# Layer 2 attention: ScalarE copies the projected queries out, high parts first in the scores, earlier folds, sums reordered, six block additions on VectorE

## The reference, cut to what matters

```python
xn = _layernorm(x)                                   # 8 x 512 x 128
# attention
xa = layernorm(xn, g1)
q = xa @ Wq.T                                        # 16 heads of 64
k, v = split(xa @ Wkv.T)                             # one head of 64, shared
q, k = l2norm(q * 16) * 4, l2norm(k) * 4
attn = softmax(causal(q @ k.T))                      # 16 x 512 x 512
x = x + layernorm((attn @ v) @ Wout.T, g2) + ffn(xn)
# ffn: (silu(xn @ Wg.T) * (xn @ Wu.T)) @ Wd.T, hidden 384
```

## Time and profile before

| what | value |
|---|---|
| time, median of 3 runs | 1253.22 us (1252.53 to 1253.65) |
| the profiled execution | 1259.26 us, its span 1257.5 us |
| PE, DVE, ACT, POOL busy in the span | 1158.6, 884.8, 670.3, 484.8 us |
| mean granted clock of TensorE | 0.978 of full speed |
| layer 2 | from about 622 us to the end, 8 turns |

### The profile page before, as it was taken

One profiled execution on the slowest core, in us unless ns is written; L12 is line 12 of the kernel. 1 busy time (PEld: TensorE's weight loads), 2 busy tenths in 40 slices (PEclk: granted clock), 3 DMA queues, 4 the chain that ended last, 5 costly groups with the idle time before them and its releaser, 6 DMA issues.

```text
span 1257.5 us, 26722 instructions
## 1 busy us (share of the span) xinstructions
PE 1158.6 (92%) x8667; PEld 789.6 (63%) x8667; DVE 884.8 (70%) x2425; ACT 670.3 (53%) x1290; POOL 484.8 (39%) x691
## 2 busy tenths in 40 slices
PE   5999999999999998898499999999999999999997
PEld 3656656665666654888365757657576575765755
DVE  7888888888888895554475767757677576775744
ACT  2766676667667655454263552635526355263550
POOL 5222212122222312553373572735727357273450
PEclk8999999999999998899699999999999999999998
DMA  3311112120101100222012030120301203012030
GB/s 91 100 47 39 56 26 57 27 70 17 27 17 27 26 10 1 55 58 51 10 23 39 13 54 6 23 38 13 54 4 25 38 13 54 4 25 38 9 52 9
DMA packets 43717, 42.31 MB, mean 34 GB/s; under 512 B 7040, under 2 KB 36224, under 8 KB 43648
## 3 DMA queue, kind: packets, MB, share of 16 engines
q0 software_dynamic: 11008, 17.31, 7.9%
q1 hardware_dynamic: 32640, 24.15, 7.1%
HBM read 13.72 MB, written 6.75 MB: 16 GB/s over the span
## 4 chain that ended last, share of the span: by engine, by line
issue 18%; PE 11%; POOL 7%; DMA 5%; ACT 5%; DVE 5%; POOLq 0%; ACTq 0%; DVEq 0%
DMA arena<-arena 5%; PE gather L496 4%; PE ring_a L496 3%; PE pair L496 3%; ACT arena L1510 3%; POOL arena L1286 3%; POOL arena L1207 2%; POOL q_len L1248 1%; DVE q_parts L1994 1%; POOL late L1286 1%; ACT arena L1490 1%; ACT q_parts L1498 1%; DVE arena L2068 1%; PE ring_d L496 1%; PE pair L500 1%
## 5 line engine op out<-in xcount | busy, mean ns | idle before, releaser
L1353 ACT ACTIVATE arena<-ring_a 128x384 f32<-128x384 f32 (+1 forms) x512 | 253.6, 550 | 148.4 <-PE ring_a L496 148.4
L1102 POOL TENSOR_SCALAR_AFFINE_SELECT arena<-arena 128x512 f32<-128x512 f32 x128 | 82.8, 647 | 367.5 <-ACT arena L1353 367.4
L496 PE MATMUL ring_a<-q_max,rows 128*128 128x384 f32 (+1 forms) x512 | 197.5, 389 | 2.2 <-DVE q_max L1659 1.8
L1645 DVE CUSTOM_DVE_ANT_0 arena<-pair,arena 128x384 bf16<-128x384 f32 (+1 forms) x269 | 161.0, 613 | 23.6 <-PE pair L496 19.2
L1510 ACT ACTIVATE arena<-ring_a 128x1024 f32<-128x1024 f32 x96 | 98.8, 1029 | 105.3 <-PE ring_a L496 105.3
L1248 POOL TENSOR_TENSOR q_len<-q_sum,exponents 128x8 f32<-128x8 f32 x64 | 105.5, 1649 | 111.3 <-DVE q_sum L1975 111.0
L496 PE MATMUL ring_a<-q_parts,k_rows 64*128 64x384 f32 (+2 forms) x1152 | 124.8, 339 | 16.0 <-DVE q_parts L1994 15.2
L496 PE MATMUL ring_a<-arena,v_aug 128*32 128x384 f32 (+1 forms) x1024 | 124.3, 557 | 1.7 <-POOL arena L1102 0.6
L496 PE MATMUL pair<-arena,v_aug 128*64 128x512 f32 (+3 forms) x768 | 114.0, 439 | 4.1 <-ACT arena L1510 3.5
L496 PEld LDWEIGHTS ring_a<-q_parts,k_rows 64*128 64x128 f32 x1152 | 92.2, 186 | 35.0 <-issue 15.8
L496 PE MATMUL pair<-rows,q_rows 128*128 128x384 f32 (+1 forms) x269 | 110.0, 411 | 3.4 <-DMA rows<-k_rows 2.6
(11 more groups left out here) (274 smaller groups left out, 2353.5 us busy)
## 6 DMA issues: line engine op xcount, KB each, us to landing
arena<-arena POOLq DMA_DIRECT2D x32, 384.0 KB, 4.4
rows<-k_rows SPq DMA_DIRECT2D x128, 64.0 KB, 2.0
arena<-in_w SPq DMA_DIRECT2D x16, 256.0 KB, 2.8
slots_y<-arena SPq DMA_DIRECT2D x39, 64.0 KB
x_all<-in_x SPq DMA_DIRECT2D x8, 256.0 KB, 4.0
tokens_x<-xn SPq DMA_DIRECT2D x8, 256.0 KB, 2.6
out<-o_t SPq DMA_DIRECT2D x8, 256.0 KB, 2.3
arena<-tokens_x,tokens_now POOLq DMA_INDIRECT x40
```

What stands on the lines that cost most here:

```text
L496: return pe.matmul(out, lhs, rhs, start=start, stop=stop, skip_group_check=True)
L1102: pool.affine_select(out=v, in_=v, compare_op=ALU.is_ge, fill=0.0, base=0, pattern=[[0, HG], [1 if late else -1, P]], channel_multiplier=- ...
L1353: act.activation(probs[:, t % NT, h, 0:many], A.slot(("cols", c))[:, 0:many], ACT.Exp).then_inc(A.free.sem, A.free.add(1))
L1645: dve.tensor_tensor_reduce(dump[:, h % 2, 0:many], M.slot(("max", n))[:, 0:many], masks[:, m, at:at + many], 1.0, LOWEST, ALU.add, ALU.max ...
```

## The change

Five parts, all in layer 2.

1. ScalarE gets one more instruction in `squares(n)`: it copies the query bank to SBUF (`q_raw`, the tensor xn_t) and frees the bank (q_free). VectorE's `q_unit` scales that copy and tells it by a new semaphore, units, for which `turn_q` waits, and for which ScalarE waits before it overwrites the copy.
2. `scores(n)` no longer waits for q_lo at its head. It waits for q_hi (the freed transpose bank; for n = 0 "moved" 4), does the two products with q_hi of blocks 1 and 3, then waits for q_lo and does the third.
3. `fold(n - 2)` at the head of step n on GpSimd, in place of `fold(n - 3)` at its end.
4. `sums1(1)` is done in step 6 before `turn_q(7)`, not in step 7; `sums1(2)` in step 7, not in step 6.
5. VectorE adds blocks 1, 2, 3 into block 0 of pairs 4 and 5 (`add_blocks`, six additions in step 6), and `sums1(2)` does block 0 alone.

```diff
@@ -809,7 +810,7 @@
                     if n < 2:
                         pe.wait_ge(SR["r_free"].sem, SR["R"].emptied(b, ("q", n)))
                     else:
-                        pe.wait_ge(Q.free.sem, Q.emptied(b, ("q", n)))
+                        pe.wait_ge(s["units"].sem, s["units"].at(b, n - 1))
                     pe.wait_ge(S.free.sem, S.fillable(b, ("q.T", n)))
                     turn(S.slot(("q.T", n)), lambda i: two_heads(n, i)).then_inc(S.full.sem, S.full.add(1))
@@ -820,17 +821,35 @@
                                   start=(last == 0), stop=(last == 2)) for c in range(2)]
                     return ins[-1]
-                def scores(n):
-
-                    pe.wait_ge(s["q_lo"].sem, s["q_lo"].at(b, n + 1))
-                    pe.wait_ge(M.free.sem, M.fillable(b, ("probs", n, 0)))
-                    sl = M.slot(("probs", n, 0))
-                    side_by_side([sl[:, c * T:c * T + 384] for c in range(2)], 1, n)
-                    side_by_side([sl[:, c * T + 384:c * T + 512] for c in range(2)], 3, n).then_inc(M.full.sem, M.full.add(1))
+                def part_of(outs, j, n, k_part, q_part, start=False, stop=False):
+
+                    return [mm(outs[c], k_stack[of_half(c), k_part, j * P:(j + 1) * P], q_part[of_half(c), n % QB, j * P:T],
+                               start=start, stop=stop) for c in range(2)][-1]
+
+                def middle_scores(n):
+
                     pe.wait_ge(S.free.sem, S.fillable(b, ("probs", n, 1)))
                     if n > 1:
                         pe.wait_ge(O.free.sem, O.emptied(b, ("o", n - 2)))
                     side_by_side([bank[:, 0:256] for bank in (S.slot(("probs", n, 1)), banks_d[1])], 2, n).then_inc(S.full.sem, S.full.add(1))
+
+                def scores(n):
+
+                    if n:
+                        pe.wait_ge(S.free.sem, S.emptied(b, ("q.T", n)))
+                    else:
+                        pe.wait_ge(SR["moved"].sem, SR["moved"].at(b, 4))
+                    pe.wait_ge(M.free.sem, M.fillable(b, ("probs", n, 0)))
+                    sl = M.slot(("probs", n, 0))
+                    one, three = [sl[:, c * T:c * T + 384] for c in range(2)], [sl[:, c * T + 384:c * T + 512] for c in range(2)]
+                    part_of(one, 1, n, 0, q_hi, start=True)
+                    part_of(one, 1, n, 1, q_hi)
+                    part_of(three, 3, n, 0, q_hi)
+                    part_of(three, 3, n, 1, q_hi)
+                    pe.wait_ge(s["q_lo"].sem, s["q_lo"].at(b, n + 1))
+                    part_of(one, 1, n, 0, q_lo)
+                    part_of(three, 3, n, 0, q_lo, stop=True).then_inc(M.full.sem, M.full.add(1))
+                    middle_scores(n)
                     pe.wait_ge(W.free.sem, W.fillable(b, ("probs", n, 2)))
                     sl = W.slot(("probs", n, 2))
                     side_by_side([sl[:, c * T:c * T + 512] for c in range(2)], 0, n).then_inc(W.full.sem, W.full.add(1))
@@ -855,7 +874,9 @@
                         pe.wait_ge(s["g_free"].sem, s["g_free"].at(b, 0))
                     if m < N_FOLD // 2:
                         pe.wait_ge(s["folded"].sem, s["folded"].at(b, 32 * (m + 1)))
-                    for j in (0, 2, 3) if m < N_FOLD // 2 else range(NT):
+                    if m == 2:
+                        pe.wait_ge(s["added4"].sem, s["added4"].at(b, 6))
+                    for j in ((0, 2, 3), (0, 2, 3), (0,), range(NT))[m]:
                         for h in range(HG):
                             ins = mm(gather[32 * h:32 * h + 32, j * P:T], pick_sum[:, m, :], p_of(2 * m + h // 2, h % 2, j),
                                      start=(m == 0 and j == 0), stop=(m == NP // 2 - 1 and j == NT - 1))
@@ -870,14 +891,18 @@
                     scores(n)
                     if n + 2 < NP:
                         project_q(n + 2)
+                    if n == 6:
+                        sums1(1)
                     if n + 1 < NP:
                         turn_q(n + 1)
                     if n + 1 < HC:
                         gate_up(n + 1)
                     if n:
                         values1(n - 1)
-                        if n in (5, 6, 7):
-                            sums1((0, 2, 1)[n - 5])
+                    if n == 5:
+                        sums1(0)
+                    if n == 7:
+                        sums1(2)
                 values1(NP - 1)
                 if not last:
                     turn_x(b + 1)
@@ -1271,10 +1296,13 @@
                 s["folded"].restart()
                 for n in range(NP):
+                    if 0 <= n - 2 < N_FOLD:
+                        fold(n - 2)
                     if n + 2 < NP:
                         q_length(s, n + 1, b)
                     p = probs1[n % PB]
-                    for third, ring in enumerate((s["M"], s["S"], s["W"])):
+                    for third in (0, 1, 2):
+                        ring = (s["M"], s["S"], s["W"])[third]
                         pool.wait_ge(ring.free.sem, ring.emptied(b, ("probs", n, third)))
                         apart(pool)
                         if third == 0:
@@ -1286,8 +1314,6 @@
                             ins = pool.affine_select(out=v, in_=v, compare_op=ALU.is_ge, fill=0.0, base=0,
                                                      pattern=[[0, 2], [1, P]], channel_multiplier=-1)
                         ins.then_inc(s["masked"].sem, s["masked"].add(1))
-                    if 0 <= n - 3 < N_FOLD:
-                        fold(n - 3)
                     if not last and n == 0:
                         fetch_slots(b + 1)
                     if not last and n in (1, 2):
@@ -1481,6 +1507,8 @@
                         act.wait_ge(s["sums"].sem, s["sums"].at(b, n - 2))
                     act.activation(q_sq.rearrange("p g d -> p (g d)"), Q.slot(("q", n))[:],
                                    ACT.Square).then_inc(s["squared"].sem, s["squared"].add(1))
+                    act.wait_ge(s["units"].sem, s["units"].at(b, max(n - 2, 0)))
+                    act.activation(q_raw[n % 2], Q.slot(("q", n))[:], ACT.Copy).then_inc(Q.free.sem, Q.free.add(1))
                 def gate_up(c):
                     act.wait_ge(W.full.sem, W.filled(b, ("gu", c)))
@@ -1511,7 +1539,7 @@
                 gate_up(0)
                 for n in range(NP):
-                    for third in range(3):
+                    for third in (0, 1, 2):
                         exp_of(n, third)
                     if n + 2 < NP:
                         squares(n + 2)
@@ -1983,10 +2011,15 @@
                     dve.wait_ge(SR["r_full"].sem, SR["R"].filled(b, "q.T"))
                 elif n > 2:
                     dve.wait_ge(SC["s_full"].sem, SC["S"].filled(b, ("q.T", n - 2)))
+                if s is SR:
+                    raw, made = ring.slot(("q", n))[:, :], ring.free
+                else:
+                    dve.wait_ge(ring.free.sem, ring.emptied(b, ("q", n)))
+                    raw, made = q_raw[n % 2], s["units"]
                 dve.scalar_tensor_tensor(
-                    out=q_nat[n % 2], in0=ring.slot(("q", n))[:, :].rearrange("p (g d) -> p g d", d=D1), scalar=QSCALE1 * ROOT_SCALE,
+                    out=q_nat[n % 2], in0=raw.rearrange("p (g d) -> p g d", d=D1), scalar=QSCALE1 * ROOT_SCALE,
                     in1=q_rn[:, half].unsqueeze(2).to_broadcast([P, 2 * NT, D1]), op0=ALU.mult,
-                    op1=ALU.mult).then_inc(ring.free.sem, ring.free.add(1))
+                    op1=ALU.mult).then_inc(made.sem, made.add(1))
             def q_low(n):
@@ -2010,7 +2043,7 @@
             def attend(b, last):
                 s = SC
                 O, L, S, W, Z = (s[k] for k in "OLSWZ")
-                for name in ("q_free", "o_free", "l_free", "e_free", "own", "var", "sums", "q_lo", "h1", "g_free", "inverted", "fin"):
+                for name in ("units", "o_free", "l_free", "e_free", "own", "var", "sums", "q_lo", "h1", "g_free", "inverted", "fin", "added4"):
                     s[name].restart()
                 for name in () if last else ("r_free", "own", "var", "xn", "xa", "sums", "k_n", "added"):
                     SR[name].restart()
@@ -2030,7 +2063,18 @@
                     dve.wait_ge(ring.full.sem, ring.filled(b, ("o", n)))
                     dve.tensor_copy(o1[:, n, :], ring.slot(("o", n))[:]).then_inc(ring.free.sem, ring.free.add(1))
+                def add_blocks(n):
+
+                    dve.wait_ge(O.full.sem, O.filled(b, ("o", n)))
+                    for j in range(1, NT):
+                        dst = probs_of(n, 0)[:, :, j * P:T]
+                        dve.tensor_tensor(dst, dst, probs_of(n, j), ALU.add).then_inc(s["added4"].sem, s["added4"].add(1))
+                        if j < NT - 1:
+                            dve.wait_ge(s["added4"].sem, s["added4"].at(b, s["added4"].n))
+
                 for n in range(NP):
+                    if n == 6:
+                        add_blocks(4)
                     if n + 2 < NP:
```

(2 more changed lines are left out.)

11 lines of the change are left out of this document (6 added, 5 removed).

## The result

The changed kernel takes **1245.57 us**, median of 19 runs (1241.51 to 1254.31), beside 1255.55 for the kernel before in 19 runs on the same chip (1252.06 to 1264.15). The ratio is 0.9929, 95% interval 0.9912 to 0.9946: faster by 0.7%, about 9 us. I had said 1231.4, with a range of 1223 to 1243. The sign was right and the size was not: less than half of the 21.8 us came.

The account below looks back on a forecast made before the run. PE's own work plus its waits bound a layer 2 turn; seven turns at 2.5 us and 4.3 for the last gave 21.8 off the median 1253.22, so 1231.4 us, range 1223 to 1243.

Parts of the forecast that it names:

- Fewer sums: sums1(2) keeps 4 of 16 matmuls: PE drops 1.40 us per turn; VectorE's additions, about 2.4 per pair, cost nothing.
- High parts first: Start of scores(n), S(n), mostly needs only q_hi: S(0) 0.7 us sooner, S(1) 0.8, S(3) and S(4) 0.95.
- ScalarE's copy: project_q(6) loses its 0.97 us wait; turn_q(5) then waits 0.6 for q_unit(5), still 1.45 sooner than before.
- Sooner folds: On GpSimd the roots end at 976.2 instead of 977.44; fold(3) is issued there and lands 4.4 us later.
- the term of -2.9 per turn: All parts together over one layer 2 turn: 2.9 us less, before 0.4 for VectorE's SBUF operand left 2.5.
- Sums ahead of turn_q(7): sums1(1) waits 1.0 us for fold(3), in place of 0.58 before turn_q(7); S(7) comes 2.15 sooner.
- VectorE's new operand: q_unit reads both inputs from SBUF while GpSimd masks: 0.2 us for each of two q_units, 0.4 per turn.
- The last turn: Layer 2's last turn, without fetches and roots: waits for fold(1) and before turn_q(7) go, 4.3 us less.
- (A): Rival: GpSimd and the fold bind harder, fold(3) landing in 5.7 us or a tensor_scalar locked out; about 1240; chance 0.15.
- (D): Rival: fold(3) in time, so no wait of 1.0 us at sums1(1); 7 us more gain, 1224; chance 0.1.
- (B): Rival: the shared port makes it slower, every q_unit 1.1 us late behind its step's masks; 1262 us; chance 0.08.

Follow-up runs that it names:

- roots_later: Changed kernel with the next batch's roots moved from the end of step 4 to step 5, behind fold(3) and q_length(7); 1235.76 us, ratio 0.9846.
- gathers_211: roots_later with the next batch's four gathers issued two in step 0, one in step 1, one in step 2; 1222.86 us, ratio 0.9887.

## Why the prediction failed, step by step

*Fewer sums*: right. 1.30 per turn for 1.40, and the additions of a pair took 2.27 to 2.33 in most turns for my 2.4, with nobody waiting.

*High parts first*: right to S(3) (S(0) -0.68 for -0.7, S(1) -0.75 for -0.8, S(3) -0.9 for -0.95). S(4) came -0.7 in the better turns and -0.6 in the others for my -0.95, since turn_q(4) was late. The part is worth about 0.1 us of a turn once GpSimd bounds turn_q(5).

*ScalarE's copy*: the wait at project_q(6) went, and the new one at turn_q(5) was 0.39 to 1.50 for my 0.6. In turns two to seven turn_q(5) began 30.29 from the turn's beginning twice, 30.91 three times and 31.49 once, where I had 29.99. Three terms of that walk were off. The second gather was to end 0.7 sooner than before; it ended 1.1 sooner in the two better turns and 0.2 in the others, where ScalarE had waited 0.3 at its square and the selects took 1.95. Fold and power took 3.14 (881.29 to 884.43) for my 3.0. And q_unit(5) took 1.7 to 2.3 for my 1.5, since its tensor_scalar took 0.48 to 1.09 for 0.36. The selects at q_unit(4) show the second of these cases. First the kernel before, then both kinds of turn of the changed one:

```profile
959.04 1.48 POOL L1286 TENSOR_SCALAR_AFFINE_SELECT arena<-arena 128x256 f32<-128x256 f32 x4
```

```profile
953.73 1.56 POOL L1314 TENSOR_SCALAR_AFFINE_SELECT arena<-arena 128x256 f32<-128x256 f32 x4
...
876.59 1.95 POOL L1314 TENSOR_SCALAR_AFFINE_SELECT arena<-arena 128x256 f32<-128x256 f32 x4
...
881.29 1.43 POOL L1294 DMA_DIRECT2D arena<-arena  x1
882.12 2.31 POOL L1273 TENSOR_TENSOR q_len<-q_sum,exponents 128x8 f32<-128x8 f32 x1
```

```profile
953.97 1.35 DVE L1961 TENSOR_SCALAR q_len<-q_len 128x8 f32<-128x8 f32 x1
...
876.83 0.20 DVE L1961 TENSOR_SCALAR q_len<-q_len 128x8 f32<-128x8 f32 x1
...
877.47 0.80 DVE L2019 SCALAR_TENSOR_TENSOR q_nat_sb<-xn_t,q_rn 128x512 f32<-128x512 f32 x1 [0.21 <-DVE q_rn L1963]
```

In the turn of 932.86 VectorE was held for 1.35 and GpSimd's four selects took 1.56; in the turn of 855.32 VectorE was let through, its scaling (877.47, both inputs in SBUF) fell inside the selects, and they took 1.95. Before the change the scaling read PSUM, fell inside the selects too (it began at 959.84) and they took 1.48. Of the changed kernel's two, the first is the turn with the wait of 0.39, the second that of 0.91.

*Sooner folds* **is the step that failed**: it took the roots, and with them fold(3), as 1.2 us sooner than before because q_unit(6) would be. VectorE's statistics ended 0.45 sooner in the two better turns (970.28, 974.53 in the times of before, against 974.98) and 0.4 later in the usual ones, and fold(3) was issued at 976.97 and at 977.8 for 976.2. Two things held q_unit(6) up: its sum stands on VectorE behind q_unit(5) and the two instructions of the next batch's expert addition, so that the lateness of the step above is passed on, and its power took 2.04, having begun inside a q_low. The fold landed 4.5 behind its issue, as forecast. At sums1(1) the wait was 1.40 to 1.43 for 1.0 in every turn but the first, and what turn_q(5) had lost stood in front of it. I had also left the first turn out, where the wait is 2.2 to 3.1. So the term of -2.9 per turn, of which I took back 0.4 for the port, came to about -1.0 in the usual turns and -1.9 in the better ones.

*Sums ahead of turn_q(7)*: right as an order, and its price is the row above. With the fold in time (roots_later) it is the best part of the change.

*VectorE's new operand*: 0.08 more on L2019 (means 773 and 742 ns for 691) and 0.08 in front of it, against my 0.2. What I left out is the other side: the selects, 397 to 401 ns each at the median before, became 466 (arena) and 850 (late) in turns two to seven. I had priced the port on VectorE alone. The rule that I cited from the Trainium skill, SBUF — State Buffer ("Practical consequences"), that the first starter holds the pair for its instruction, names both engines; this trace agrees in part. The selects grew by 0.4 us where VectorE's scaling with two inputs in SBUF fell inside them, and not where it read PSUM. But in both turns above the tensor_scalar, which has one tensor input, came 0.24 us after the first select; once it ran at once, once it was held until all four selects had ended, and not one.

*The last turn*: 5.4 for 4.3. Some 1.1 of it is the granted clock: behind the same idle 1.90 it was 0.58 from 1239 to 1243 before, near the lower of its two levels (1.2 GHz), and 1.00 (2.4 GHz) at the same place now.

Of the rivals, (A) has the right title, GpSimd and the fold bind harder, and a price of 7 to 9 us, which gave 1240; it had 0.15. Its two causes were not what happened in most turns: fold(3) landed in 4.5 and not in 5.7 (5.2 in the first turn), and a tensor_scalar of 1.09 stood in front of turn_q(5) in one turn of seven. That its number came near is in part luck. (D) needed the order of roots_later. (B) came only in small: q_unit(5) took 0.2 to 0.8 more than I had, where it wanted 1.1 at each.

## What to carry to other kernels

When an engine's queue is in a loop with PE, price every instruction of that queue between two of its waits, with the length that it has beside its new neighbour on the other engine, before taking any wait off PE: here 2.8 us of waits went from a usual turn, and 2.3 came back at two places, turn_q(5) and sums1(1). Look for the small instruction in front of a long transfer's issue; moving three of them behind it gave 9 to 14 us, where the five parts together had given 6 to 10. And run the old kernel on a second chip before believing a wait that depends on the phase of two engines.

The fastest order found is gathers_211_no_copy: parts 2 to 5 of the change with the roots behind fold(3), the gathers two, one, one, and no copy; 0.9873 (0.9844 to 0.9902) and 0.9889 (0.9868 to 0.9911) of the kernel before, in two groups on one chip where that takes 1236 to 1238. It leads gathers_211 by 2.3 us, with intervals that overlap. Where the kernel before takes 1255 it wasn't run; roots_later has 0.984 there.

## What the runs showed of the hardware

A power of 8 columns on GpSimd took 1.62 to 1.71 us with VectorE idle and no fold's issue just in front (430 of 430) and 2.02 to 2.21 when it began with 0.5 us or more of a VectorE subtraction ahead that reads both inputs from SBUF (71 of 71). The issue of an accumulating DMA took 1.2 to 1.4 on GpSimd, and the row of the instruction behind it began up to 0.6 before the issue's row ended: in the changed kernel issue and power together were 3.0 to 3.1, about their sum. Four selects of 128 x 256 took 1.49 alone and 1.95 beside a VectorE pass of 512 columns with two inputs in SBUF. A VectorE tensor_scalar of 8 columns that began 0.18 or 0.24 us into four selects took 0.20 to 0.25 in some turns and 1.33 to 1.35 in others, in two executions of one kernel as in two turns of one execution. The same kernel stood at 1255 and 1236 us on different chips, with turns of 78.6 and 77.2 at the same granted clock of 1.00. In those turns the square of the queries of pair 4 is 0.54 sooner and that 8-column instruction is held or not; by S(5) the two traces are 1.56 apart, of which 0.5 was there before the instruction. What makes the stretch ahead of layer 2 9.7 us shorter there was not looked into.
